# Two-layer kernel: shared experts with weights stationary over 512 tokens, and first routed weights loaded during the attention

## The reference

```
n = layernorm(x)
x = x + selective_ssm(n)                  # 16 states, scan over 1024 tokens
      + top-1 of 8 experts(n)             # inner size 176, weighted
n = layernorm(x)
x = x + attention(n)                      # 16 heads, causal, semantic + rotary parts, values of 128
      + sum over the top 4 of 60 experts  # inner size 176
            weight * (silu(n @ gate.T) * (n @ up.T)) @ down.T
      + sigmoid(n @ shared_gate.T)        # shared, inner size 704
            * (silu(n @ g.T) * (n @ u.T)) @ d.T
```

## Time and profile before

| | us |
|---|---|
| median of 3 runs | 2059.88 (2059.81 to 2061.33) |
| the profiled execution, whole | 2061.09 |
| its span | 2059.5 |
| PE busy | 1834.8 (89%) |
| DVE busy | 1147.2 (56%) |
| ACT busy | 984.2 (48%) |
| POOL busy | 781.8 (38%) |

### The profile page before, as it was taken

How to read it: one execution, slowest core, us unless ns; L and a number is a source line. 1 busy time by engine, 2 the same in 40 slices (tenths; PEclk the granted TensorE clock), 3 DMA queues, 4 the chain that set the end, 5 groups by cost and what they waited for, 6 DMA issues and landing times.

```text
span 2059.5 us, 34795 instructions
## 1 busy us (share of the span) xinstructions
PE 1834.8 (89%) x9258; PEld 1353.7 (66%) x9258; DVE 1147.2 (56%) x2241; ACT 984.2 (48%) x2152; POOL 781.8 (38%) x768
## 2 busy tenths in 40 slices
PE   7139999556999999999999999999997999999998
PEld 3125566345777777777777777777775777777775
DVE  3888884577464546454555555555543343443665
ACT  3139993214555555555555555555552444443222
POOL 1138892413443434343434343434340222222333
PEclk9559999757999999999999999999998999999999
DMA  9112228510000000000000000000004999998334
GB/s 392 48 58 102 102 92 260 156 40 9 19 16 20 8 18 15 20 10 15 20 15 19 9 18 15 20 8 18 8 11 123 325 321 313 330 320 276 106 104 127
DMA packets 108967, 201.17 MB, mean 98 GB/s; under 512 B 16468, under 2 KB 68948, under 8 KB 106484
## 3 DMA queue, kind: packets, MB, share of 16 engines
q1 hardware_dynamic: 70212, 132.95, 20.4%
q0 software_dynamic: 17408, 48.39, 7.2%
q10 hardware_dynamic: 21312, 19.41, 2.8%
HBM read 140.78 MB, written 51.51 MB: 93 GB/s over the span
## 4 chain that ended last, share of the span: by engine, by line
PE 70%; DVE 13%; issue 7%; ACT 6%; DMA 1%; POOL 1%; DVEq 1%; ACTq 0%; SPq 0%; POOLq 0%
PE ps L761 13%; PE ps L540 12%; PE ps L568 9%; PE ps L736 6%; PE ps L1459 5%; PE ps L754 4%; PE ps L697 4%; PE ps L699 4%; PE ps L698 4%; DVE xr L966 3%; DVE negmax L934 3%; PE ps L1453 3%; ACT sw L866 3%; PE ps L530 2%; PE ps L548 2%
## 5 line engine op out<-in xcount | busy, mean ns | idle before, releaser
L1046 POOL TENSOR_TENSOR sw<-sw,rope_t 64x512 f32<-64x512 f32 x128 | 164.3, 1284 | 613.3 <-ACT sw L866 613.3
L949 DVE TENSOR_TENSOR t<-ps,rope_t 128x512 f32<-128x512 f32 x128 | 88.5, 692 | 365.2 <-ACT sw L866 365.1
L761 PE MATMUL ps<-pt,v 128*128 128x512 f32 (+3 forms) x768 | 270.1, 495 | 19.9 <-DVE xr L966 17.8
L858 ACT ACTIVATE pb<-ps,negmax 128x128 f32<-128x128 f32 (+7 forms) x256 | 190.8, 745 | 179.2 <-DVE negmax L934 179.1
L540 PE MATMUL ps<-w13r,xt 128*128 128x352 f32 x752 | 254.8, 461 | 0.0
L934 DVE TENSOR_REDUCE negmax<-ps 128x1 f32<-128x128 f32 (+7 forms) x256 | 192.1, 750 | 77.5 <-PE ps L720 75.3
L613 DVE SCALAR_TENSOR_TENSOR ga<-th,ps 128x176 f32<-128x176 f32 x212 | 71.6, 338 | 282.0 <-ACT th L584 245.5
L761 PEld LDWEIGHTS ps<-pt,v 128*128 128x128 f32 x768 | 139.0, 191 | 121.4 <-issue 79.4
L568 PE MATMUL ps<-w2r,ht 88*128 88x256 f32 x848 | 217.8, 379 | 0.0
L509 POOL DMA_DIRECT2D w2r<-in_w x148 | 77.2, 522 | 335.9 <-PE ps L568 288.1
L754 PE MATMUL ps<-ident,pb 128*128 128x128 f32 x1152 | 171.3, 276 | 23.8 <-ACT pb L858 23.6
(11 more groups left out here) (179 smaller groups left out, 3591.1 us busy)
## 6 DMA issues: line engine op xcount, KB each, us to landing
w13r<-in_w SPq DMA_DIRECT2D x128, 352.0 KB, 5.0
w2r<-in_w POOLq DMA_DIRECT2D x152, 176.0 KB, 4.9
result<-yy ACTq DMA_DIRECT2D x148, 128.0 KB, 4.7
sorted<-zeros SPq DMA_DIRECT2D x18, 1024.0 KB, 21.1
crow<-c_rows SPq DMA_DIRECT2D x32, 512.0 KB, 3.6
xs<-sorted SPq DMA_DIRECT2D x124, 128.0 KB
hc<-in_w SPq DMA_DIRECT2D x24, 352.0 KB, 5.6
xs<-xn SPq DMA_DIRECT2D x64, 128.0 KB
```

What stands on the lines that cost most here:

```text
L761: last = pe.matmul(ps[:, 6, c0:512], v[:, buf, j], pt[g][:, j, c0:512], start=j == 0, stop=j == 4 * g + 3)
L858: act.activation(pb[:, qt % 2, 0:cols], ps[:, bank:bank + 2, :].rearrange("p a n -> p (a n)")[:, 0:cols], ACT.Exp, bias=negmax[:, par, qn: ...
L1046: g.tensor_tensor(sw[64:128, p % 2, :], sw[64:128, p % 2, :], rope_t[64:128, 1, (p // 2) * 512:(p // 2 + 1) * 512], ALU.mult).then_inc(s_t ...
```

## The change

The shared experts leave the ring. Their weights are loaded in one piece each (`sh_raw13`, `sh_raw2`, together 2.23 MB) by SyncE when the attention has ended, and GpSimd splits them in ten pieces between the loads of down weights of the routed tiles. After the routed tiles come 24 units: four blocks of 512 tokens by six chunks of 128 hidden features (the last has 64). In a unit PE multiplies the chunk's gate and up weights, as the stationary side, with 512 columns of `xnr` and `xnl`, which gives the hidden values already transposed; ScalarE takes tanh, VectorE gates, ScalarE rounds the product and VectorE takes the rest; PE then multiplies each of four token tiles of it with the chunk's down weights and adds up over the six chunks in PSUM. No tokens are loaded or transposed for this, and 64 tiles with their instructions go. VectorE adds three gathered rows in each unit, and a block's sums after the block's last down product. Gate and up of unit 0 are issued after the drain of the routed pipeline.

In layer 1 the ring's weight buffers no longer lie over the attention's, and the token buffers share space with `t1`: the first four gate and up weights and down weights are loaded once the routing table is known, the first four token tiles once the rotations and scatters are over. In both layers SyncE issues the first four weight loads ahead of the first four token loads. Semaphores of stores and gathers are shared by the layers.

```diff
-SHARED = 4
+SHARED_H = 704
+SHC = -(-SHARED_H // P)
+SHB = T // 512
 TILES0 = T // P + E0
 TILES1 = T * K1 // P + E1
-ALL1 = TILES1 + SHARED * NT
...
+        t1 = sbk("t1", [P, 2, 512])
+        early = {"w13r1": sbk("w13r1", [P, RING, DC, 2 * INNER]), "w2r1": sbk("w2r1", [IC, RING, 2, D]),
+                 "xs1": t1[:].rearrange("p a (b d) -> p (a b) d", d=D)}
...
+        ring_buffers(R1, 1, lambda n, sh, dt=F32: early[n] if n in early else sbm(n, sh, dt))
+        sh_raw13 = sbm("sh_raw13", [P, DC, 2 * SHARED_H])
+        sh_raw2 = sbm("sh_raw2", [P, SHC, D])
+        sh13 = [sbm(f"sh13_{k}", [P, DC, 2 * SHARED_H], F32R) for k in range(2)]
+        sh2 = [sbm(f"sh2_{k}", [P, SHC, D], F32R) for k in range(2)]
...
-        def experts_sp(sp, r):
-        def experts_pool(g, r):
+        def load_w13(sp, r, i, q):
+            s = i * RING + q
+            e = sp.value_load(r.etab[0:1, bass.ds(s, 1)], min_val=0, max_val=r.n_weights - 1)
+            w(sp, r.gu_ready, s - 3)
+            sp.dma_start(r.w13[:, q], r.w13_dram[bass.ds(e, 1)].rearrange("o p c n -> (o p) c n")).then_inc(r.w13_loaded[q], 16)
+        def load_tokens(sp, r, i, q):
+            s = i * RING + q
+            w(sp, r.gu_ready, s - 3)
+            sp.dma_start(r.xs[:, q], r.slots[bass.ds(s * P, P), :]).then_inc(r.x_loaded[q], 16)
+        def experts_sp(sp, r, first_tokens=lambda: None, then=lambda: None):
+            for q in range(RING):
+                load_w13(sp, r, 0, q)
+            first_tokens()
+            for q in range(RING):
+                load_tokens(sp, r, 0, q)
+            then()
+            with sp.Fori(1, r.tiles_n // RING) as i:
+                for q in range(RING):
+                    load_tokens(sp, r, i, q)
+                    load_w13(sp, r, i, q)
+        def load_w2(g, r, i, q):
+            s = i * RING + q
+            e = g.value_load(r.etab[0:1, bass.ds(s, 1)], min_val=0, max_val=r.n_weights - 1)
+            w(g, r.dn_done, s - 3)
+            g.dma_start(r.w2[:, q], r.w2_dram[bass.ds(e, 1)].rearrange("o p c n -> (o p) c n")).then_inc(r.w2_loaded[q], 16)
+        def experts_pool(g, r, extra=()):
+                load_w2(g, r, 0, q)
+            for i, do in enumerate(extra):
+                do()
-        def experts_pe(pe, r):
+                    load_w2(g, r, 1 + i, q)
+            with g.Fori(1 + len(extra), r.tiles_n // RING) as i:
+                for q in range(RING):
+                    load_w2(g, r, i, q)
+        def experts_pe(pe, r, near_end=None):
...
+        UNITS = SHB * SHC
+        def rows_of(n):
+            return min(P, SHARED_H - (n % SHC) * P)
+        def shared_banks(n):
+            return 2 * (n % 2), 2 * (n % 2) + 1
+        def total_bank(block, tile):
+            return 4 + 2 * (block % 2) + tile // 2, slice((tile % 2) * D, (tile % 2 + 1) * D)
+        def split_piece(g, m, src, hi, lo):
+            g.tensor_copy(hi, src).then_inc(s_shr, 1)
+            g.wait_ge(s_shr, m + 1)
+            g.tensor_tensor(lo, src, hi.bitcast(F32), ALU.subtract).then_inc(s_shs, 1)
+        SHARED_SPLITS = 2 * DC * 2 + 2
+        def shared_splits(g):
+            def first():
+                g.wait_ge(s_shw, 32)
+            def piece(m):
+                if m < 2 * DC * 2:
+                    sl = (slice(None), m // 4, slice((m % 4) * 352, (m % 4 + 1) * 352))
+                    split_piece(g, m, sh_raw13[sl], sh13[0][sl], sh13[1][sl])
+                else:
+                    sl = (slice(None), slice((m % 2) * 3, (m % 2) * 3 + 3))
+                    split_piece(g, m, sh_raw2[sl], sh2[0][sl], sh2[1][sl])
+            return [lambda: None, first] + [lambda m=m: piece(m) for m in range(SHARED_SPLITS)]
+        def shared_gate_up(pe, n):
+            rows, block, j = rows_of(n), n // SHC, n % SHC
+            w(pe, s_shh, n - 1)
+            for part in range(2):
+                cols = slice(part * SHARED_H + j * P, part * SHARED_H + j * P + rows)
+                toks = slice(block * 512, (block + 1) * 512)
+                for c in range(DC):
+                    last = three(pe, ps[0:rows, shared_banks(n)[part], :], sh13[0][:, c, cols], sh13[1][:, c, cols],
+                                 xnr[:, c, toks], xnl[:, c, toks], c == 0, c == DC - 1)
+            last.then_inc(s_shgu, 1)
+        def shared_down(pe, n):
+            rows, block, j = rows_of(n), n // SHC, n % SHC
+            if j == 0 and block >= 2:
+                pe.wait_ge(R1.shared_added, (block - 1) * 4)
+            pe.wait_ge(s_shhl, n + 1)
+            for tile in range(4):
+                bank, cols = total_bank(block, tile)
+                toks = slice(tile * P, (tile + 1) * P)
+                o = ps[:, bank, cols]
+                hr, hl = sh_hr[0:rows, n % 2, toks], sh_hl[0:rows, n % 2, toks]
+                wr2, wl2 = sh2[0][0:rows, j], sh2[1][0:rows, j]
+                pe.matmul(o, hr, wr2, start=j == 0 and tile % 2 == 0, stop=False, skip_group_check=True)
+                pe.matmul(o, hl, wr2, start=False, stop=False, skip_group_check=True)
+                last = pe.matmul(o, hr, wl2, start=False, stop=j == SHC - 1, skip_group_check=True)
+            last.then_inc(s_shdn, 1)
+        def shared_pe(pe):
+            for n in range(1, UNITS + 1):
+                if n == 1:
+                    pe.wait_ge(R1.h_done, TILES1)
+                    pe.wait_ge(R1.y_copied, TILES1)
+                if n < UNITS:
+                    shared_gate_up(pe, n)
+                shared_down(pe, n - 1)
+        def shared_act(act):
+            for n in range(UNITS + 1):
+                if n < UNITS:
+                    act.wait_ge(s_shgu, n + 1)
+                    w(act, s_shg, n - 1)
+                    rows = rows_of(n)
+                    act.activation(sh_th[0:rows, n % 2], ps[0:rows, shared_banks(n)[0], :], ACT.Tanh, scale=0.5).then_inc(s_sht, 1)
+                if n:
+                    m = n - 1
+                    rows = rows_of(m)
+                    act.wait_ge(s_shh, m + 1)
+                    w(act, s_shdn, m - 1)
+                    act.copy(sh_hr[0:rows, m % 2], sh_h[0:rows, m % 2]).then_inc(s_shhr, 1)
+        def shared_dve(v):
+            done = [0]
+            def add_results(count):
+                for n in range(done[0], min(done[0] + count, NT * K1)):
+                    i, k = n // K1, n % K1
+                    v.wait_ge(R1.gathered[n % 4], 16 * (n // 4 + 1) + R1.gathered_before)
+                    w(v, R1.added, n)
+                    if 4 * added_blocks[0]:
+                        v.wait_ge(R1.shared_added, 4 * added_blocks[0])
+                    v.scalar_tensor_tensor(xr[:, i, :], R1.got[:, n % 4, :], R1.weight[:, i, k:k + 1], xr[:, i, :],
+                                           ALU.mult, ALU.add).then_inc(R1.added, 1)
+                    done[0] = n + 1
+            added_blocks = [0]
+            def add_block(block):
+                v.wait_ge(s_shdn, SHC * (block + 1))
+                w(v, R1.added, done[0])
+                for tile in range(4):
+                    i = 4 * block + tile
+                    bank, cols = total_bank(block, tile)
+                    v.scalar_tensor_tensor(xr[:, i, :], ps[:, bank, cols], R1.weight[:, i, K1:K1 + 1], xr[:, i, :],
+                                           ALU.mult, ALU.add).then_inc(R1.shared_added, 1)
+                added_blocks[0] = block + 1
+            for n in range(UNITS):
+                rows = rows_of(n)
+                gate, up = shared_banks(n)
+                v.wait_ge(s_sht, n + 1)
+                v.scalar_tensor_tensor(sh_ga[0:rows, n % 2], sh_th[0:rows, n % 2], 1.0, ps[0:rows, gate, :], ALU.add, ALU.mult).then_inc(s_shg, 1)
+                v.wait_ge(s_shg, n + 1)
+                w(v, s_shhr, n - 1)
+                v.scalar_tensor_tensor(sh_h[0:rows, n % 2], sh_ga[0:rows, n % 2], 0.5, ps[0:rows, up, :], ALU.mult, ALU.mult).then_inc(s_shh, 1)
+                if n:
+                    add_results(3)
+                v.wait_ge(s_shhr, n + 1)
+                w(v, s_shdn, n - 1)
+                v.tensor_tensor(sh_hl[0:rows, n % 2], sh_h[0:rows, n % 2], sh_hr[0:rows, n % 2].bitcast(F32), ALU.subtract).then_inc(s_shhl, 1)
+                if n >= SHC and n % SHC == 1:
+                    add_block(n // SHC - 1)
+            add_results(NT * K1)
+            add_block(SHB - 1)
...
+            sp.wait_ge(R0.scattered, 16 * NT)
...
-            sp.wait_ge(s_e6, use6(ITS, W3))
-            sp.wait_ge(s_e7, use7(ITS - 2, 4))
-            experts_sp(sp, R1)
+            def attention_over():
+                sp.wait_ge(s_ql, 4 * ITS)
+                sp.wait_ge(R1.scattered, 16 * NT * K1)
+            def attention_weights_over():
+                sp.wait_ge(s_e6, use6(ITS, W3))
+                sp.wait_ge(s_e7, use7(ITS - 2, 4))
+                sp.dma_start(sh_raw13[:], shared13).then_inc(s_shw, 16)
+                sp.dma_start(sh_raw2[:], shared2).then_inc(s_shw, 16)
```

(65 more changed lines are left out.)

100 lines of the change are left out of this document (36 added, 64 removed).

## The result

The changed kernel takes 2066.57 us (median of 9 runs, 2058.02 to 2071.28), the kernel before 2060.36 beside it (9 runs). The ratio is 1.0022, with an interval of 1.0013 to 1.0032, so 2.7 to 6.6 us slower. The forecast was 2062. The profiled execution took 2066.91 us, its span is 2065.0 (before 2059.5).

What follows compares the result with a forecast made beforehand. PE's own columns were taken to bound the kernel. Span 2059.5 - 6.1 (shared stage) - 6.0 (routed start with layer 0) = 2047.4, plus 1.6 around it 2049.0, plus 13 for clock falls: 2062 us, range 2045 to 2076.

Steps and rivals of the forecast that it cites:

- The gap: Shared stage: PE idles 2.35 us (2.0 to 2.7) after each gate/up, making a unit 6.59 us.
- rival (b): Shared stage: no gap, chains of two units overlap, 4.45 us a unit; 2000 us, chance 0.05.
- The clock: Shared stage: gaps make PE's clock fall about 10 times at up to 1.3 us each, +13 us.
- (a): Rival, shared stage: the clock holds at full despite the gaps; 2049 us, chance 0.30.
- (c): Rival, shared stage: clock falls at nearly every gap (2079 us) or stays low (2133); chance 0.12.
- -6.1: Shared stage to the end of the span, before clock falls: 165.1 us against 171.2.
- Layer 0: Four weight loads go ahead of tile 0's tokens: costs 0.7 us (0 to 3).
- four loads at about 1 us of issue use that up: Layer 0: issuing four weight loads uses up the 5.9 us between the tokens' issue and use.
- The start of the routed stage: Layer 1: first gate/up 7.5 us earlier, 0.3 lost to low clock, 0.5 (0 to 6.5) to tile 4's tokens.
- Rival (d): Routed stage: early weights bring nothing, tile 4 waits 6 us behind the shared weights; 2068 us, chance 0.08.
- landing in 5.0 of 8.8 us: Routed stage, tile 4's tokens: a load lands 5.0 us after issue in steady state, with 8.8 until use.
- Splits on GpSimd and the gathers: Ten splits hold down-weight loads some 1 us at most, inside slack: nothing; three gathers per unit: no cost (0 to 3).

Runs made afterwards that it cites:

- Experiment 1: Changed kernel with ScalarE's cast of unit n-1 put ahead of the tanh of unit n: 2010.06 us, ratio 0.975.
- experiment 3: Changed kernel with its gap kept but filled by extra PE matmuls in each unit: eight 2052.89 us, ratio 0.9955; four 2054.89 us, ratio 0.9967.
- experiment 8: Changed kernel with cast first, routed results behind the difference, layer 0's old order; now only 0.57 of 2.23 MB shared weights loaded: 2012.07 us, ratio 0.975.
- experiment 6's second kernel: Changed kernel with cast first, routed results behind the difference, layer 0's old order; now without layer 1's early loads: 2018.67 us, ratio 0.9783.

## Why the prediction was right in its size, and where its steps were off

**The gap: confirmed, 4 us too large.** PE waits in each of 24 units for VectorE's difference, behind a tanh and a cast, as the loops' order has it. I had 6.59 us a unit, it is 6.41; the idle time after gate/up's last slot is 1.92 + 0.16 = 2.08, not 2.35. tanh 0.597, cast 0.609, difference 0.692 stand against 0.60, 0.62 and 0.73, but the cast starts 0.494 behind the tanh's start, ahead of its end, and the three hand-overs left take 0.04, 0.03 and 0.06, not 4 x 0.05. Matmul slots are 0.233 and 0.12; a unit's downs take 1.53, not 1.44, as the first slot is 0.22. Experiment 1 shows the cause alone: rival (b)'s 2000 us needed one change of order, and that kernel is at 2010.

**The clock: confirmed.** Nine units show a fall, one of them a longer one; by their excess over units without one (6.4, with a block's adds 6.6 to 6.7) they cost 15.2 us, by experiment 3 15.0. I had 10 x 1.3 = 13; a fall costs 1.5, not 1.3. The granted clock of the stage, 0.89, is in the forecast's 0.85 to 0.95; rivals (a) and (c) are out. The count was partly luck: ten falls came from two rows, one with a fall and one without, and nothing in them gave one gap in two or three. The Trainium skill (TensorE: Matmul & The Clock Gate, A second HAM failure mode: psum-queue depth-cycling) says that small idle times between groups of matmuls can make the clock swing; 2.1 us in 6.4 did so here in nine units, 1.0 us in two, none when filled.

Both together: from gate/up of 123 to the end I had +6.9 (-6.1 + 13), the trace has +5.2.

**Layer 0: mis-sized.** I had +0.7 (0 to 3). The pair of profiles says up to +4.4 by the last projection, but over all profiled executions it is +2.4. The step that failed is "four loads at about 1 us of issue use that up": the issue took 4.10 us as said, but I treated all 5.9 us between issue and use as slack. The tokens need 4.1 of them to land (319.81 to 323.93). PE waits 1.4 us more, and the clock is low around that wait.

**The start of the routed stage: two terms too small, which cancel.** I had -7.5 + 0.3 + 0.5 = -6.7; the trace has -4.0. The early loads are worth not 7.5 but some 14 us: besides the earlier first gate/up, 8.8 us come later in the stage. That they also take 2.1 MB out of a full stage would fit, but isn't shown. And the shared weights cost more than 0.5: tile 4 waits 3.2 us with a stretch at the low clock behind it, a wait that is gone with the smaller load of experiment 8. Over the whole stage the kernel before to experiment 6's second kernel gives about 8.5, close to the 7 us that 2.23 MB need at 318 GB/s; but experiment 8 loads 1.66 MB less and gains nothing over the stage, so the size of this term stays open. Rival (d) named this place rightly; the wait was 3.2 us, not 6, and its conclusion, that the early weights bring nothing, was false. Whether its reason, that the DMA engines have no room at 1.02, holds is open: at that share transfers kept PE's beat in some traces and not in others. My reason against it (landing in 5.0 of 8.8 us) used the landing time of a single load in steady state for a queue with 7 us of work put ahead.

The errors, -4, +2, +2 and +3 us in the order of these parts, are of both signs and add to +3; the rest of the 4.6 us between forecast and median is within what the kernels vary by. Splits on GpSimd and the gathers cost nothing visible, as said.

The time fell where I had thought it less likely: over 2064.0, my own limit for slower, had 0.33, faster 0.40, since I gave a clock that holds 0.30. The range held it and the mechanisms were the right ones, but the closeness of 2062 owes something to the count of falls and to errors of both signs.

## What to carry over

Where two engines pass a value back and forth in a software pipeline, write for each engine's loop which instruction of unit n stands ahead of which of unit n-1: an instruction of n-1 behind one that needs unit n's matmuls gives a gap in every unit, here 2.1 us of 6.4 and, with the clock, 56 us in all. And in a stage with a DMA share of 1.0, the landing time of a load in steady state (5.0 us here) is no measure of what it can stand behind: tokens queued behind 2.23 MB came 3.2 us too late. What such bytes cost over the whole stage has to be measured: 1.66 MB less won 4.3 us up to tile 4 and lost 10.2 behind it.

## What the runs showed of the hardware beyond that

- A PE that does more runs faster: eight extra 0.23 us matmuls in each 6.4 us unit saved 13.7 us, through the granted clock.
- The routed stage, at a DMA share of 1.02 to 1.05, runs from tile 4 to 123 in 296 to 308 us in different kernels and executions (without those that load the shared weights late, with a wait in it), with 320 to 322 GB/s between 1600 and 1880 us in the short ones and 309 to 317 in the long ones, and gate and up weights landing 4.6 us after issue in the shortest, 6.3 in the longest.
- A cast on ScalarE starts 0.494 us behind the start of a tanh that takes 0.597, in each of 23 units.
- ScalarE was 3.2 to 3.6 us late at three places of one kernel (and up to 2.4 and 3.2 in two related ones) with its operand ready and nothing in the trace that held it, and in none of the ten other kernels traced.
